# Expert results added in DRAM by indirect DMAs, instead of stored in five rows a token and added on TensorE

## The reference, cut to what matters

```
score = sigmoid(norm(x) @ gate_w)           # 16 experts
top   = the 4 experts with the largest score + gate_b
w     = score[top] / sum(score[top]) * 2.5
y     = shared(norm(x)) + sum over the 4 of w[e] * expert_e(norm(x))
out   = x + layernorm(y)
expert_e(v) = (silu(v @ w1_e) * (v @ w3_e)) @ w2_e      # 256 -> 128 -> 256
```

## Time and profile before

| | us |
|---|---|
| median of 3 runs | 2382.17 (2374.33 to 2387.48) |
| profiled execution, its own time | 2401.79 |
| its span, first to last instruction | 2400.0 |
| tile stage, 2033 to 2299 | 266 |
| last pass, 2299 to 2400 | 101 |

### The profile page before, as it was taken

One profiled execution on the slowest core, in us unless ns is written; L12 is line 12 of the kernel. 1 busy time (PEld: TensorE's weight loads), 2 busy tenths in 40 slices (PEclk: granted clock), 3 DMA queues, 4 the chain that ended last, 5 costly groups with the idle time before them and its releaser, 6 DMA issues. The chain is left out here.

```text
span 2400.0 us, 32259 instructions
## 1 busy us (share of the span) xinstructions
PE 1863.6 (78%) x10562; PEld 1175.3 (49%) x10658; DVE 1587.9 (66%) x3257; ACT 840.8 (35%) x1772; POOL 784.5 (33%) x627
## 2 busy tenths in 40 slices
PE   0877998898799789789978988987665343888867
PEld 0544454554455445445544545544343342878743
DVE  3224697589569658856966985795698363666635
ACT  0243343344235334333523433442321132555410
POOL 0000144134214304321430431242178644555521
PEclk9678998999899999889989999999876665999989
DMA  4000000000000000000000000000122245455476
GB/s 130 0 1 9 1 1 10 11 1 1 19 1 1 9 10 1 1 19 1 1 9 10 1 10 10 1 1 9 36 92 86 90 152 198 148 155 155 145 273 238
DMA packets 82707, 122.92 MB, mean 51 GB/s; under 512 B 12697, under 2 KB 69341, under 8 KB 82400
## 3 DMA queue, kind: packets, MB, share of 16 engines
q1 hardware_dynamic: 68944, 84.39, 11.2%
q0 software_dynamic: 13056, 35.68, 4.0%
q10 hardware_dynamic: 528, 0.52, 0.1%
HBM read 69.81 MB, written 52.84 MB: 51 GB/s over the span
## 5 line engine op out<-in xcount | busy, mean ns | idle before, releaser
L650 DVE TENSOR_TENSOR_SCAN s_buf<-r_work,kvb 128x512 f32<-128x512 f32 x256 | 351.0, 1373 | 1.1 <-POOL p_buf L828 1.0
L828 POOL TENSOR_TENSOR p_buf<-s_buf,r_work 128x512 f32<-128x512 f32 x128 | 152.6, 1192 | 453.9 <-DVE s_buf L650 446.5
L904 ACT ACTIVATE probs<-bank_s,nmx 128x256 f32<-128x256 f32 (+1 forms) x512 | 186.6, 450 | 110.2 <-DVE nmx L513 109.0
L828 POOL TENSOR_TENSOR r_work<-s_buf,r_work 128x512 f32<-128x512 f32 x128 | 158.6, 1241 | 198.2 <-DVE s_buf L650 197.9
L793 POOL TENSOR_TENSOR rstd<-vare,mhalf 128x4 f32<-128x4 f32 x48 | 48.4, 1008 | 458.4 <-DVE vare L446 458.3
L922 ACT ACTIVATE pt<-bank_s 128x1024 f32<-128x1024 f32 (+1 forms) x128 | 117.5, 918 | 219.4 <-PE bank_s L1212 219.4
L639 DVE TENSOR_TENSOR kvb<-r_work,bank 128x512 f32<-128x512 f32 x256 | 174.5, 682 | 20.2 <-PE bank L1330 11.7
L1860 POOL DMA_INDIRECT y_rows<-w_in_ys,m_y_idx x144 | 141.7, 984 | 137.9 <-ACT w_in_ys L1938 96.9
L513 DVE TENSOR_REDUCE nmx<-bank_s 128x4 f32<-128x1024 f32 (+1 forms) x128 | 137.6, 1075 | 48.5 <-PE bank_s L1162 48.3
L1329 PE MATMUL bank<-v_hi,sel_v 128*128 128x512 f32 x256 | 129.3, 505 | 18.1 <-DVE kvb L639 11.4
L1054 PE MATMUL bank_s<-wmask,ident_b 128*128 128x512 bf16 x340 | 102.4, 455 | 51.2 <-DVE vare L446 32.7
(11 more groups left out here) (393 smaller groups left out, 4256.1 us busy)
## 6 DMA issues: line engine op xcount, KB each, us to landing
m_xs<-x_rows SPq DMA_DIRECT2D x146, 144.0 KB
w_lo<-y_rows SPq DMA_DIRECT2D x4, 2560.0 KB
w_hi<-y_rows SPq DMA_DIRECT2D x4, 2560.0 KB
w_in_ys<-in_w SPq DMA_DIRECT2D x17, 256.0 KB
x_new<-in_x SPq DMA_DIRECT2D x8, 512.0 KB, 3.7
x_after_rwkv<-x_b SPq DMA_DIRECT2D x8, 512.0 KB, 3.8
m_x_tok<-x_after_rwkv SPq DMA_DIRECT2D x6, 512.0 KB, 4.4
y_rows<-pt SPq DMA_DIRECT2D x5, 512.0 KB, 3.2
```

The costliest lines, as they stand in the source:

```text
L650: V.tensor_tensor_scan(s_buf[:, n % 2, 1:S + 1], dec[:, n // HD, :], kvb[:, n % 2, :], 0.0, ALU.mult, ALU.add).then_inc(sem["state"], 1)
L828: G.tensor_tensor(p_slot(n), s_buf[:, n % 2, 0:S], rf[:, n // HD, :], ALU.mult).then_inc(sem["rs"], 1)
L904: ins = A(probs[:, n % 2, x, h * w:h * w + w], score_banks[n % 2][:, x, h * w:h * w + w], ACT.Exp, bias=nmx[:, n, 2 * x + h:2 * x + h + 1])
```

## The change

The array of five rows a token is replaced by two arrays `y_acc[0]` and `y_acc[1]` with one row a token, and 128 further rows for the rows that only fill up tiles. The shared expert's result is stored into `y_acc[0]`, and `y_acc[1]` is filled with zeros by a DMA from SP in the row stage. The indirect DMA of tile s adds its rows to `y_acc[s % 2]` (`compute_op=ALU.add`). A token can occur in two tiles that go to one array, so POOL waits before the DMA of tile s until the DMA of tile s - 2 has landed. A token needs only one index now, and the scan that counted its experts goes. The x rows of all batches are kept in or loaded into SBUF during the row and tile stages (`x_all`). In the last pass SP loads two rows a token instead of five, DVE adds them, and the work is spread out over engines: DVE sums and takes statistics, POOL takes the root, ACT normalises, DVE adds x; DVE does the sum of batch b, the mean of b - 1 and the addition of b - 2 in turn. PE has no part in it any more.

```diff
-YK = TOPK + 1
+ACCS = 2
-    y_rows = nc.dram_tensor("y_rows", (B * S * YK, D), F32, kind="Internal").ap()
+    y_acc = [nc.dram_tensor(f"y_acc{n}", (B * S + P, D), F32, kind="Internal").ap() for n in range(ACCS)]
...
 # row stage, SP of mid_token_layers, ahead of the loop over the batches
+            sp.wait_ge(e_const, 3)
+            for n in range(1, ACCS):
+                sp.dma_start(y_acc[n][0:B * S].rearrange("(p a n) d -> p a (n d)", p=P, a=B), e_zeros.unsqueeze(1).broadcast_to((P, B, NT * D))).then_inc(e_loaded, 16)
+            for n in range(ACCS):
+                sp.dma_start(y_acc[n][B * S:B * S + P], e_zeros[:, 0:D]).then_inc(e_loaded, 16)
...
 # row stage, place_rows, DVE
-                own.link(V.tensor_tensor_scan(flat(count[:]), flat(reset[:]), flat(mask[:]), 0.0, ALU.mult, ALU.add))
-                V.tensor_tensor(xr[b % 2][:, :, D + NE:ROW].bitcast(U32), count[:], y_row[:], ALU.add)
+                V.tensor_copy(xr[b % 2][:, :, D + NE].bitcast(U32), y_row[:])
...
 # tile stage, SP
             for g in range(1, N_GROUPS):
+                if g <= EARLY:
+                    sp.dma_start(x_all[:, g - 1], rows(x3[g - 1:g])).then_inc(x_in[0], 16)
...
 # tile stage, POOL
             def rows_to_tokens(s, g, u):
                 gp.wait_ge(sem[("y_kept", "y_odd")[u % 2]], ...)
-                G.indirect_dma_start(y_rows, bass.IndirectOffsetOnAxis(y_idx[:, u % Y_RING:u % Y_RING + 1], 0), ys[:, u % Y_RING, :], None,
-                                     bounds_check=B * S * YK - 1, oob_is_err=False).then_inc(ys_out[u % Y_RING], 16)
+                if s >= ACCS:
+                    last = s - ACCS
+                    gp.wait_ge(ys_out[last % Y_RING], 16 * (last // Y_RING + 1))
+                G.indirect_dma_start(y_acc[s % ACCS], bass.IndirectOffsetOnAxis(y_idx[:, u % Y_RING:u % Y_RING + 1], 0), ys[:, u % Y_RING, :], None,
+                                     compute_op=ALU.add).then_inc(ys_out[u % Y_RING], 16)
...
 # last pass, SP
+            for b in range(B):
+                for n in range(ACCS):
+                    sp.dma_start(y_in_sb[n][b], of_batch(y_acc[n], b)).then_inc(y_loaded(b), 16)
             for b in range(B):
                 sp.wait_ge(sem["x_final"], b + 1)
-                sp.dma_start(rows(out[b:b + 1]), x_end[b % RING]).then_inc(sem["x_out"], 16)
+                sp.dma_start(rows(out[b:b + 1]), x_all[:, b]).then_inc(sem["x_out"], 16)
...
 # last pass, DVE
+            def end_sum(b):
+                ve.wait_ge(y_loaded(b), y_in(b))
+                if b >= 2:
+                    ve.wait_ge(sem["y_normed"], b - 1)
+                own.link(V.tensor_tensor(y_total[b % 2], y_in_sb[0][b], y_in_sb[1][b], ALU.add))
+                for i in range(NT):
+                    ins = V.bn_stats(st[:, i, :], y_total[b % 2][:, i, :])
+                own.link(ins, tick)
+                for i in range(NT):
+                    ins = V.bn_aggr(end_mv[:, b % 2, i, :], st[:, i, :])
+                own.link(ins)
+                V.tensor_scalar(end_vare[:, b % 2], end_mv[:, b % 2, :, 1], EPS, None, ALU.add).then_inc(sem["var"], 1)
+            def end_mean_of(b):
+                ve.wait_ge(sem["rstd"], LATE + b + 1)
+                V.scalar_tensor_tensor(end_mean[:, b % 2], end_mv[:, b % 2, :, 0], -1.0, end_rstd[:, b % 2], ALU.mult, ALU.mult).then_inc(sem["y_mean"], 1)
+            def end_add(b):
+                if b == 0:
+                    ve.wait_ge(x_in[0], 16 * (len(range(0, LATE, 2)) + EARLY))
+                ve.wait_ge(sem["y_normed"], b + 1)
+                V.tensor_tensor(x_all[:, b], x_all[:, b], yn[b % 2], ALU.add).then_inc(sem["x_final"], 1)
+            for b in range(B + 2):
+                if b < B:
+                    end_sum(b)
+                if 0 < b <= B:
+                    end_mean_of(b - 1)
+                if b > 1:
+                    end_add(b - 2)
...
 # last pass, ACT
+            for b in range(B):
+                sc.wait_ge(sem["y_mean"], b + 1)
+                if b >= 2:
+                    sc.wait_ge(sem["x_final"], b - 1)
+                for i in range(NT):
+                    ins = A(yn[b % 2][:, i, :], y_total[b % 2][:, i, :], ACT.Identity, bias=end_mean[:, b % 2, i:i + 1], scale=end_rstd[:, b % 2, i:i + 1])
+                ins.then_inc(sem["y_normed"], 1)
...
 # last pass, PE
-            for b in range(B):
-                pe.wait_ge(xs_in[b % RING], all_in(b))
-                if b >= 2:
-                    pe.wait_ge(sem["x_final"], b - 1)
-                for h in range(2):
-                    o = bank[2 * (b % 2) + h]
-                    for k in range(YK):
-                        ins = T.matmul(o[:], ident[:], y4[b % RING][:, 2 * h:2 * h + 2, k, :], start=k == 0, stop=k == TOPK)
-                    ins.then_inc(sem["y_sum"], 1)
```

More of the change, by code:

```diff
@@ L114, in program @@
     x_rows = nc.dram_tensor("x_rows", (N_ROWS + P, ROW), F32, kind="Internal").ap()
-    y_rows = nc.dram_tensor("y_rows", (B * S * YK, D), F32, kind="Internal").ap()
-    with nc.sbuf_tensor("before", [P, NE], F32) as before:
-        mid_token_layers(nc, t, x3, x_rows, y_rows, before)
-        expert_layer(nc, t, x3, x_rows, y_rows, before, out)
+    y_acc = [nc.dram_tensor(f"y_acc{n}", (B * S + P, D), F32, kind="Internal").ap() for n in range(ACCS)]
+    with ExitStack() as ctx:
+        before = ctx.enter_context(nc.sbuf_tensor("before", [P, NE], F32))
+        rows_out = [ctx.enter_context(nc.semaphore(f"rows_out{i}")) for i in range(2)]
+        y_out = [ctx.enter_context(nc.semaphore(f"y_out{i}")) for i in range(2)]
+        mid_token_layers(nc, t, x3, x_rows, y_acc, before, rows_out, y_out)
+        expert_layer(nc, t, x3, x_rows, y_acc, before, rows_out, y_out, out)
 class Own:
@@ L270, in e_tile @@
             return ap if len(shape) == 1 else ap.rearrange("p (a c) -> p a c", c=shape[1])
+        e_zeros = pt[:, 1].rearrange("p x s -> p (x s)")
         e_re = e_tile(NT * NE)
-        e_score, e_comb, e_mask, e_first, e_reset, e_count, e_key, e_y_row = (e_tile(NT, NE) for _ in range(8))
+        e_score, e_comb, e_mask, e_first, e_key = (e_tile(NT, NE) for _ in range(5))
+        e_y_row = e_tile(NT)
         e_biased, e_rest = e_tile(NT, NE + TOPK), e_tile(NT, NE + TOPK)
@@ L705, in expert_rows @@
                 V.memset(before[:], 0.0)
-                own.link(V.memset(e_reset, 1.0))
-                V.memset(e_reset[:, :, 0], 0.0)
+                for i in range(2):
+                    V.memset(e_xr[i][:, :, D + NE:ROW], 0.0)
+                V.memset(e_zeros, 0.0).then_inc(e_const, 1)
                 own.link(V.tensor_scalar(e_tri, e_tri, 0.0, None, ALU.is_equal))
@@ L1432, with expert_layer @@
 )
-PER4 = dict(y_odd=1, y_sum=2, x_final=1, x_out=16)
-def expert_layer(nc, t, x3, x_rows, y_rows, before, out):
+PER4 = dict(y_odd=1, y_mean=1, y_normed=1, x_final=1, x_out=16)
+def expert_layer(nc, t, x3, x_rows, y_acc, before, rows_out, y_out, out):
     with ExitStack() as ctx:
@@ L1504, in expert_layer @@
         table = sb("m_table", [1, 4, 160], I32)
-        x_tok = [sb(f"m_x_tok{i}", [P, NT, D]) for i in range(2)]
+        x_all = sb("m_x_all", [P, B, NT, D])
+        x_tok = [x_all[:, b] for b in range(EARLY, B)]
         xr = [sb(f"m_xr{i}", [P, NT, ROW]) for i in range(2)]
@@ L1636, in _ @@
             V.memset(biased[:, :, NE:], BIG)
-            V.memset(xs[:, GROUP - 1, 0:D + NE], 0.0)
-            V.memset(xs[:, GROUP - 1, D + NE:ROW], 1.0)
+            own.link(V.memset(xs[:, GROUP - 1, :], 0.0))
+            for i in range(2):
+                V.memset(xr[i][:, :, D + NE:ROW], 0.0)
             V.memset(tiles[:, 2, :], 1.0)
             V.memset(table[:].rearrange("p a n -> p (a n)"), 0)
-            own.link(V.memset(reset[:], 1.0))
-            V.memset(reset[:, :, 0], 0.0)
             own.link(V.tensor_scalar(tri[:], tri[:], 0.0, None, ALU.is_equal))
@@ L1808, in _ @@
             y_odd(TILES - 1, GROUP - 1)
-            def end(b):
-                o = lambda i: bank[2 * (b % 2) + i // 2][:, (i % 2) * D:(i % 2) * D + D]
+            def end_sum(b):
[3 more added lines that the diff above has]
+                own.link(V.tensor_tensor(y_total[b % 2], y_in_sb[0][b], y_in_sb[1][b], ALU.add))
+                for n in range(2, ACCS):
+                    own.link(V.tensor_tensor(y_total[b % 2], y_total[b % 2], y_in_sb[n][b], ALU.add))
```

118 lines of the change are left out of this document (49 added, 69 removed).

## The result

The changed kernel takes 2439.66 us (median of 4 runs, 2434.95 to 2442.94), the kernel before 2382.14 us on the same chip (2374.33 to 2387.48). The ratio is 1.022, with a 95% interval of 1.0188 to 1.0252: it is slower by 57.5 us, where 21 us of gain had been forecast. The two profiled executions have spans of 2441.1 and 2400.0 us. They differ by 41.1 only, because the profiled execution of the kernel before was 19.6 us above its median and that of the changed kernel 3.3.

The account below looks back on a forecast made before the run. PE and its hand-offs were taken to bound the tile stage, PE the last pass after its first load. 2401.8 - 47 - 1.6 + 23 + 5 - 1 = 2380 us profiled, so a median of 2361; range 2332 to 2440.

Parts of the forecast that it names:

- the part that decides: Tile stage: POOL's wait for the scatter two tiles back, free only while a round stays below 3.59 us; +23 us.
- three rivals: Whole kernel: free wait, 2332 us, chance 0.15; scatters bind, 2470, 0.32; last pass slow, 2370, 0.08.
- the scatter chain becomes the bound: Tile stage: rival, read ahead of write makes the round 5.43 us, +132 instead of +23, 2470 us; chance 0.32.
- Last pass as it becomes: Last pass: from the last landing 49 us instead of 96.2, bound by DVE; gain 47, between 38 and 50.
- the case with gaps: Last pass: rival, DVE still waits for the root, 58 us rather than 49, total 2370; chance 0.08.
- The landing before it: Last scatter: lands 3.6 us after its start instead of 5.18, as x loads move forward; -1.6 us.
- Tile stage, the added wait: Tile stage: waiting for scatter s - 2 makes a round of 3.91 us, 1.955 a tile against 1.795; +23 us.
- 0.29 us to spare: Tile stage: margin of a plain scatter's round, 3.3 us, below two tiles at the old pace, 3.59 us.
- The adding part of the same step: Tile stage: adding instead of storing lengthens the round by 0.26 and 0.35 us, from 3.3 to 3.91.
- Tile stage, x loads: Tile stage: five 0.5 MB loads slow the scatters by 1 us each; +5 us, bounds 0 and 11.
- Filler rows: Tile stage: rows added to spare rows instead of dropped, at most 16 experts' last tiles; nothing.
- row stage: Stage before the tiles: scan and addition go, a copy comes, -1 us; zeros cost nothing, 13 us if not covered.

Follow-up runs that it names:

- e2_plain_rows: The changed kernel with scatters that store instead of adding, same order and wait: 2362.80 us, ratio 1.0086 to the kernel before.
- c0_before_again: The kernel before, unchanged, profiled a second time: 2337.92 us.
- e6_wait_only: The kernel before with only the wait for the scatter of tile s - 2 added: 2408.19 us, ratio 1.0290 to the kernel before.
- c1_after_again: The changed kernel, unchanged, run again on the second chip: 2435.05 us against 2334.15 for the kernel before, ratio 1.0417.
- e3_one_array: The changed kernel with all scatters adding to one array, each waiting for the previous one: 2751.11 us, ratio 1.1743 to the kernel before.
- e1_three_arrays: The changed kernel with three arrays in turn instead of two, waiting for the scatter three back: 2373.64 us against 2341.01 for the kernel before, ratio 1.0129.

## Why the prediction was wrong

The mechanism that I called "the part that decides" did decide. Its size was wrong, and of the forecast and its three rivals "the scatter chain becomes the bound" came true: the round is 4.87 us, above the 4.2 from which it was said to eat the gain, and below the 5.43 of that case. The steps in their order:

- **"Last pass as it becomes", 49 us: right in mechanism, 6.5 too low.** Measured 55.5 from the landing. The first sum starts 5.9 us after it (forecast 5), and a batch takes 5.56, not 4.83. The root is not what DVE waits for, as the case with gaps had it; it waits 1.07 a batch for ACT. Two rows had been carried over at their old length: the root takes POOL 1.98 us in six of the eight batches, against 1.01, and a normalisation on ACT 0.59, against 0.39. Gain 40.7, inside the bounds of 38 to 50.
- **"The landing before it", -1.6: right**, -1.7.
- **"Tile stage, the added wait", +23: the step that failed**, in the round of a plain scatter first. The wake-up: I took 0.30 us, which is the gap between two scatters that wait for nothing. After a landing it is 0.7, in every chain above. The landing of 3.0 us, from one early scatter, was right as a median (3.0 in e2_plain_rows and in c0_before_again), but one value stood for all: 3.0 + 0.7 makes 3.7, and the slow landings bring the mean round to 3.91 (e2_plain_rows) and 3.96 (e6_wait_only), against 3.3 forecast. The "0.29 us to spare" were not there. On the chip where the tile takes 1.478 the wait costs 72 us. At the first trace's pace it would be 143 x (1.981 - 1.795) = 27 us before anything is added, an estimate that takes the 1.981 to hold there too.
- **The adding part of the same step, 0.26 + 0.35 = 0.61 us a round: too small.** Measured is 4.87 to 4.94 (first trace, c1_after_again) against 3.91 to 3.96, so 0.9 to 1.0. The instruction gives 1.56 - 0.98 = 0.58 of it, which I had put at nothing in the chosen value, with 0.98 more as the upper end. The median landing goes from 3.0 to 3.8 or 3.9 in all, so if the instruction's 0.58 is in it in full, 0.2 to 0.3 are left for the transfer itself, less than the 0.61. In time the part is 143 x (2.435 - 1.981) = 65 us, with the same reservation and with what the x loads cost (next point) in it. Wait, addition and x loads together are 92 us, against 23 + 5 = 28 forecast. The difference of 64 us is as good as the whole error between the traces, 62.7 us (+41.1 instead of -21.6); the medians are 16 us further apart, because the two profiled executions stood 19.6 and 3.3 us above theirs.
- **"Tile stage, x loads", +5: fits, not shown apart.** In the changed kernel the first 27 scatters, in whose time the five loads are issued, come every 2.64 us and the others every 2.39; in c1_after_again it is 2.58 and 2.45. e6_wait_only has the wait but not the loads, and there the first 27 are the faster ones, 1.89 and 2.00. An excess of 0.13 to 0.25 us over 27 tiles is 3 to 7 us. No run takes the loads out of the changed kernel.
- **"Filler rows", 0; "row stage", -1, zeros covered: right for the zeros.** They land after 12.2 us and nothing waits for them; the stretch 1700 to 1750 shows them as 0.27 of DMA (0.06 in the earlier trace rows). The first scatter stands 8 us earlier, but 5 of these are there at 1670 already, ahead of the first instruction that the change adds to this stage (1693), and on the second chip it is 3.9. I take them for the spread between executions, which no run shows. The filler rows have no visible cost: with the wait and plain stores a tile takes 1.954 us where they are stored (e2_plain_rows) and 1.981 where they are dropped (e6_wait_only).

e6_wait_only gives the price of the wait that additions need, 74 us. The Trainium skill (DMA: Bandwidth & Descriptors, Rules for kernel authors) had named that need: an accumulating DMA has to wait for the semaphore of an earlier one that touches the same bytes. That additions get lost without it, no run here shows. From the same page (Two DMAs through the same engine are not ordered) I had concluded that additions overlap row by row and so cost little. The page gives no time for this, and overlap of rows says nothing of how long the instruction holds POOL and the packets hold the DMA engines; that is what the runs show to have grown.

The chance of 0.32 for the chain was too low for another reason: the margin on which the forecast lived was 0.29 us out of 3.59, built from two single rows. When a bound rests on so small a difference of two estimates, either side is about as likely.

## What to carry to other kernels

A wait put in front of a queue of DMAs turns hidden latency into a rate: take landing plus wake-up, divide by the number in flight, and compare it with the interval between issues; if it isn't clearly below, the wait costs at least the difference in every step, whatever the share of busy DMA says. Take the mean and the slow landings from the stage itself, not one landing, and the wake-up from a scatter that did wait. Keep enough in flight that the quotient is well below: with additions, one gave 4.66 us a tile, two 2.44 to 2.47, three 1.95 and eight 1.865, which is POOL's own pace. If a pass at the end is bound by how much it reads, first move its independent loads forward; that alone gave 14 us here.

## What the runs showed of the hardware

- An indirect DMA of 128 rows of 1 KB that adds holds POOL for 1.56 us; one that stores, 0.96 to 0.98.
- It holds the 16 DMA engines about three times as long, and has three times the packets. The queue carries 128 scatters of the row stage too, so the two rows are of the tile stage alone (queue: packets, MB, share of 16 engines), the changed kernel from 2025 to 2390 and e2_plain_rows from 2015 to 2310:

```profile
q0 software_dynamic: 20736, 18.88, 45.0%
```

```profile
q0 software_dynamic: 6912, 18.88, 17.2%
```

For each of the 144 scatters these are 144 packets and 1.14 us (45.0% of 365 us) of the 16 engines with additions, 48 packets and 0.35 us (17.2% of 295 us) without. The Trainium skill (Collectives: The Full Stack, The bandwidth ceiling: the fold count and why AG ≠ RS ≠ AR) has two source reads in place of one for an addition in a ring of large chunks, and a ratio of 1.93 between the bandwidths without and with it. The factor here, on an indirect DMA of 1 KB rows, is 3.
- From the landing of a DMA to the start of the next scatter that waited for it: 0.7 to 0.8 us, of which 0.69 to 0.71 stand in the chain as one piece. Between two scatters without such a wait: 0.30.
- The landing of an adding scatter has a median of 3.8 us with one in flight, 3.9 with two and 4.5 with three (e3_one_array, c1_after_again, e1_three_arrays).
- One kernel, two traces from two chips: 1.795 and 1.478 us a tile, with PE the busiest engine in both. A pace read off one trace may not hold on the next chip.
